# Centred context as 32-column weights, key weights split once for two context groups, three key banks, and a later store of the split context, in a two-layer attention and expert kernel

## The reference, cut to what matters

```python
# x, context: 16 batches of 128 rows, 512 wide
# L0 attention: q = layernorm(x), k = v = context, 16 heads, dh = 32
D = jnp.exp(log_D - max_log_D)                      # decays, lower triangle
C = (jnp.einsum('bhsd,bhtd->bhst', qh, kh) / jnp.sqrt(dh)) * D
normalizer = jnp.maximum(jnp.abs(C.sum(-1, keepdims=True)), jnp.exp(-max_log_D))
h = jnp.einsum('bhst,bhtd->bhsd', C / (normalizer + EPS), vh)
mu = h.mean(-1, keepdims=True)
var = ((h - mu) ** 2).mean(-1, keepdims=True)
hn = (h - mu) * jax.lax.rsqrt(var + EPS) * ln_scale
x = x + hn                                          # heads side by side
...
# L1 attention: keys of the context, 16 heads of 128, over all 16 batches
k_img = rms_norm(context @ ki_w + ki_b, nki_s)      # ki_w is 512 x 2048
```

## Time and profile before

| | |
|---|---|
| median of 3 runs (lowest, highest) | 1386.42 us (1383.04, 1388.37) |
| profiled execution, its own time | 1384.88 us |
| span in its trace, first to last instruction | 1383.2 us |
| PE, share of the span busy | 96% |
| DVE, ACT, POOL | 60%, 55%, 28% |
| heads stage in the trace | 194 to 492 us |

### The profile page before, as it was taken

The page is one execution under the profiler, slowest core; times in us unless marked ns, Lnnn a source line. Parts: engine busy times, 40 slices in busy tenths (PEclk is TensorE's granted clock), DMA queues, the critical chain, the costliest instruction groups (busy, mean ns, idle before and its releaser), DMA issues. The chain is left out here.

```text
span 1383.2 us, 24553 instructions
## 1 busy us (share of the span) xinstructions
PE 1324.5 (96%) x7326; PEld 1108.3 (80%) x7327; DVE 836.1 (60%) x1590; ACT 764.5 (55%) x1895; POOL 392.7 (28%) x374
## 2 busy tenths in 40 slices
PE   7899998999999989989998989999989999999998
PEld 6688877888888768778886778888878888888887
DVE  3645544567677865354444568635467777777965
ACT  4334457788887542154445545544577555555551
POOL 0111022374639004569631054027101000000041
PEclk9999998999999999999999999999999999999999
DMA  9984497888788567475656887474556655555413
GB/s 305 353 320 154 175 314 256 270 266 268 259 269 266 174 192 265 167 237 172 205 153 220 302 261 223 108 244 156 184 180 172 167 155 166 155 164 157 125 35 122
DMA packets 175095, 288.33 MB, mean 208 GB/s; under 512 B 30176, under 2 KB 64736, under 8 KB 174752
## 3 DMA queue, kind: packets, MB, share of 16 engines
q1 hardware_dynamic: 149200, 231.78, 53.3%
q0 software_dynamic: 8672, 29.37, 6.6%
q10 hardware_dynamic: 17136, 26.09, 5.2%
HBM read 178.38 MB, written 108.80 MB: 208 GB/s over the span
## 5 line engine op out<-in xcount | busy, mean ns | idle before, releaser
L120 PE MATMUL banks<-of_shared_split,key_lead 128*128 128x512 f32 x256 | 109.5, 428 | 10.5 <-ACT heads_ksq L1051 5.4
L2939 ACT ACTIVATE prob<-banks,attend_row,rq 128x128 f32<-128x128 f32 x248 | 110.5, 470 | 0.0
L2952 ACT ACTIVATE attend_ol<-banks,of_attend_vbias 128x512 fp32r<-128x512 f32 x64 | 44.2, 690 | 117.0 <-PE banks L3151 117.0
L120 PE MATMUL banks<-wo,attend_ol 128*128 (+1 forms) x256 | 106.2, 415 | 0.0
L122 PE MATMUL banks<-of_shared_split,key_trail 128*128 128x512 f32 x256 | 103.5, 404 | 0.0
L121 PE MATMUL banks<-of_shared_split,key_lead 128*128 128x512 f32 x256 | 103.2, 403 | 0.0
L120 PE MATMUL banks<-queries_rows_split,queries_wl 128*128 128x512 f32 x256 | 100.9, 394 | 0.0
L122 PE MATMUL banks<-wo,attend_ot 128*128 (+1 forms) x256 | 100.7, 393 | 0.0
L121 PE MATMUL banks<-wo,attend_ol 128*128 (+1 forms) x256 | 99.9, 390 | 0.0
L122 PE MATMUL banks<-queries_rows_split,queries_wt 128*128 128x512 f32 x256 | 99.8, 390 | 0.0
L121 PE MATMUL banks<-queries_rows_split,queries_wl 128*128 128x512 f32 x256 | 99.7, 390 | 0.0
(11 more groups left out here) (395 smaller groups left out, 3671.8 us busy)
## 6 DMA issues: line engine op xcount, KB each, us to landing
mlstm_gmax<-running_max SPq DMA_DIRECT2D x36, 512.0 KB, 6.5
key_raw<-in_L_xattn_ki_w SPq DMA_DIRECT2D x32, 512.0 KB, 6.4
k_heads<-heads_key ACTq DMA_DIRECT2D x64, 256.0 KB, 4.9
q_heads<-queries_head SPq DMA_DIRECT2D x64, 256.0 KB
q_ahead<-q_heads SPq DMA_DIRECT2D x64, 256.0 KB, 4.2
of_attend_k<-k_heads SPq DMA_DIRECT2D x60, 256.0 KB, 4.0
of_attend_v<-v_heads SPq DMA_DIRECT2D x60, 256.0 KB, 3.4
sorted_rows<-of_shared_split SPq DMA_DIRECT2D x2, 5120.0 KB, 29.6
```

The costliest lines, as they stand in the source:

```text
L120: nc.tensor.matmul(out, lead_l, lead_r, start=first, stop=False)
L2939: ins = nc.scalar.activation(prob[:, j % 2, b, :], ps[:, j % 2, b * S:(b + 1) * S], ACT.Exp, bias=row[:, j % 2, 1, b:b + 1], scale=rq[:, b ...
L2952: nc.scalar.activation(ol[:, par, j, :], ps[:, 4 + j % 2, :], ACT.Identity, bias=vbias[:, bass.ds(quad_of(it) * 4 + j, 1)]).then_inc(ol_do ...
```

## The change

1. *Outputs.* The context is centred ahead: DVE takes each head's mean over the 32 columns (`context_sum`), POOL subtracts it (`value`, now a subtraction), and since the centred columns add up to zero, the last of 32 is left out and holds ones in its place. The outputs of four heads are made at once at steps 2, 6, 10 and 14 (`outputs`): the context of one head and batch is the weight, 128 rows by 32 columns, and `cmat` streams past it; the four heads write the four strips of 32 partitions of bank 0. DVE copies the bank to `heads_hT` (`gather`), PE turns it back with four transposes at the next step (`turn_heads`), ACT copies it out (`quad`). `close` puts the left-out column back as minus the sum of the others. The subtraction of the mean behind the outputs is gone.
2. *Key order.* KEYS lists 64 units of (head, group, visit). Behind the first 8 units, two heads run for one group and the next before the weights change, so weights are split 40 times (VISITS), not 64, and read from DRAM 20 times, not 32. Seven of the first eight leading parts are made by POOL (`early_lead`). OPENING has new steps.
3. *Banks.* Keys use banks 6, 7 and 1; a unit waits for the square of the unit three before it.
4. *Loads.* The split context of groups 2 and 3 comes in a burst of eight at steps 14 and 15 of the body before. Context for the heads is loaded a body earlier.
5. *Values stage.* The four stores of the split context move to units 30, 32, 34 and 36.

```diff
@@ values_and_gates, SP
-                if u % 4 == 2 and u >= 6 and u < 6 + 4 * G:
-                    g = (u - 6) // 4
+                if u % 2 == 0 and 30 <= u < 30 + 2 * G:
+                    g = (u - 30) // 2
...
@@ heads_and_keys
-    OPENING = (0, 1, 3, 5, 7, 10, 12, 15)
+    OPENING = (0, 1, 2, 3, 6, 9, 12, 15)
...
+    KEYS = [(k % 2 * HALF + 2 * p + j, g, k * HALF + 2 * p + j)
+            for k in range(G + 1) for p in range(HALF // 2) for g in (k - 1, k) if 0 <= g < G for j in range(2)]
+    VISITS = HALF * (G + 1)
+    KEY_BANKS = (6, 7, 1)
...
@@ SP, body
-                    if n >= LAG and not last:
-                        A.load_split(sp, after(g, PER)[0], n - LAG)
+                    if first and n >= LAG:
+                        A.load_split(sp, 1, n - LAG)
+                    if not first and not last and n >= PER - 2:
+                        if n == PER - 2:
+                            sp.wait_ge(product, CLOSES[g - 1] + 1)
+                        for part in range(C):
+                            A.load_split(sp, g + 1, (n - PER + 2) * C + part)
...
@@ POOL
+                if b == 0:
+                    pool.wait_ge(cmean_done, count + 1)
...
+                ins = nc.gpsimd.tensor_tensor(ctx1[:, half(g), b, :, 0:LAST_E],
+                                              ctx[:, b, :].rearrange("p (h e) -> p h e", e=DH0)[:, :, 0:LAST_E],
+                                              piece(cmean, b).unsqueeze(2).broadcast_to([P, H0, LAST_E]), ALU.subtract)
...
+            def early_lead(g, m):
+                if m:
+                    pool.wait_ge(raw_loaded[m // 2 % 2], (m // 4 + 1) * 16)
+                    if m >= 2:
+                        pool.wait_ge(product, m - 1)
+                    nc.gpsimd.tensor_scalar(A.wl[:, m % 2], raw[:, m // 2 % 2, :, m % 2 * P:(m % 2 + 1) * P], 1.0, None,
+                                            ALU.mult).then_inc(wl_done, 1)
...
@@ ACT
-            def pair(g, k):
-                act.wait_ge(pv, g * PER + 2 * k + 2)
+            def quad(g, c):
+                act.wait_ge(quad_turned, g * QUADS + c + 1)
...
+                nc.scalar.activation(hraw[:, half(g), :, 4 * c:4 * c + 4, :].rearrange("p b j e -> p b (j e)"),
+                                     ps[:, 0, :].rearrange("p (b w) -> p b w", b=GB), ACT.Copy).then_inc(h_done, 1)
...
             def weight_lead(g, m):
...
+                if u == FIRST_OF[v] and v >= HALF:
+                    if v == HALF:
+                        act.wait_ge(wl_done, HALF)
+                    act.wait_ge(product, LAST_OF[v - 2] + 1)
+                    A.weight_lead(act, KEYS[u][0], v // 4)
...
@@ DVE
+            def context_sum(g, b):
...
+                nc.vector.tensor_reduce(piece(cmean, b), ctx[:, b, :].rearrange("p (h e) -> p h e", e=DH0), AX, ALU.add
+                                        ).then_inc(csum_done, 1)
...
+            def gather(g, c):
+                dve.wait_ge(pv, g * QUADS + c + 1)
+                if g or c:
+                    dve.wait_ge(quad_turned, g * QUADS + c)
+                nc.vector.tensor_copy(hT[:], ps[:, 0, :]).then_inc(ht_done, 1)
...
@@ PE
+            def outputs(g, c):
...
+                if g or c:
+                    pe.wait_ge(h_done, g * QUADS + c)
+                pe.wait_ge(c_done, g * PER + 4 * c + 4)
                 for b in range(GB):
+                    for j in range(4):
+                        ins = nc.tensor.matmul(ps[32 * j:32 * j + 32, 0, b * S:(b + 1) * S], ctx1[:, half(g), b, 4 * c + j, :],
+                                               cmat[:, j, b, :], start=True, stop=True)
                 ins.then_inc(pv, 1)
+
+            def turn_heads(g, c):
+                pe.wait_ge(ht_done, g * QUADS + c + 1)
+                for b in range(GB):
+                    ins = nc.tensor.transpose(ps[:, 0, b * P:(b + 1) * P], hT[:, b * S:(b + 1) * S], K.ident[:])
+                ins.then_inc(quad_turned, 1)
...
             def keys(g, m):
...
+                pe.wait_ge(wt_done, v + 1)
+                if u >= 3:
+                    pe.wait_ge(ksq_done, u - 2)
...
                     keys_at(g, n, 0, keys, first)
                     if n % 4 == 2:
                         scores(g, n + 2, first)
-                    outputs(g, n, first)
+                        outputs(g, n // 4)
+                    if n % 4 == 3:
+                        turn_heads(g, n // 4)
```

More of the change, by code:

```diff
@@ L950, in add @@
                     ins.then_inc(res_done, 1)
+            def early_lead(g, m):
[5 more added lines that the diff above has]
+                                            ALU.mult).then_inc(wl_done, 1)
             def body(g, first):
                 for n in range(PER):
+                    if first and n + 1 in OPENING:
+                        early_lead(0, OPENING.index(n + 1))
                     mask(g, n + AHEAD)
-                    if 5 <= n < 8:
-                        for b in ((0,), (1, 2), (3,))[n - 5]:
-                            value(after(g, PER)[0], g + 1, b)
+                    at = n - (9 if first else 5)
+                    if g + 1 < G and 0 <= at < 3:
+                        for b in ((0,), (1, 2), (3,))[at]:
+                            value(g + 1, g + 1, b)
                     if not first:
-                        for at, step in ((3, centre), (8, scale), (10, weigh), (12, add)):
+                        for at, step in ((8, scale), (10, weigh), (12, add)):
                             if at <= n < at + 2:
@@ L1080, in _ @@
             last = G - 1
-            pair(last, PAIRS - 1)
+            quad(last, QUADS - 1)
             row_sums(last)
@@ L1173, in body @@
                 for n in range(PER):
+                    if n % 4 == 3:
+                        gather(g, n // 4)
                     decayed(g, n + 1, first)
+                    at = n - (7 if first else 3)
+                    if g + 1 < G and at in (0, 1):
+                        context_sum(g + 1, 2 * at)
+                        context_sum(g + 1, 2 * at + 1)
                     keys_at(g, n, 1, weight_trail, first)
@@ L1204, in _ @@
             divisor(last)
-            mean(last, 0)
-            finish(PER - LAG + 1)
-            mean(last, 1)
-            dve.wait_ge(mean_done, G)
-            shift(nc.vector, last, 0)
-            finish(PER - LAG + 2)
-            for b in range(1, GB):
-                ins = shift(nc.vector, last, b)
-            ins.then_inc(centred, 1)
-            finish(PER - LAG + 3)
+            close(last, 0)
+            close(last, 1)
+            for m in range(1, 4):
+                finish(PER - LAG + m)
             dve.wait_ge(row_stats.summed, EARLY)
@@ L1267, in scores @@
                             ins.then_inc(qk, 1)
-            def outputs(g, n, first):
-                if n == 0:
+            def outputs(g, c):
+                if c == 0:
                     pe.wait_ge(ctx1_done, g + 1)
-                if n % 2 == 0 and not (first and n < 4):
-                    pe.wait_ge(h_done, g * PAIRS + n // 2 - 1)
-                pe.wait_ge(c_done, g * PER + n + 1)
+                if g or c:
+                    pe.wait_ge(h_done, g * QUADS + c)
+                pe.wait_ge(c_done, g * PER + 4 * c + 4)
```

175 lines of the change are left out of this document (85 added, 90 removed).

## The result

The changed kernel takes 1377.3 us (median of four runs, 1374.94 to 1379.30) beside 1387.4 of the kernel before, run with it. The ratio is 0.9937, with a 95% interval from 0.9916 to 0.9958: some 9 us faster, where 20 were forecast.

A forecast was written before the change was run, and what follows sets the result against it. PE was taken to bound the heads stage, except its opening, bound by a POOL, ACT and DVE chain. 1384.88 - 19.4 - 3.9 + 4.5 + 1.0 + 0 - 2.1 + 0 = 1365.1, predicted as a 1367 us median; range 1358 to 1390.

The forecast's parts named there:

- rival 2: Heads stage: the chain from transposes over ACT to the trailing part replaces the outputs as bound; about 1381 us, chance 0.21.
- Opening: First body of the heads stage: late second key unit against cheaper outputs and relieved ACT; taken as 0, bounds -8 and +6.
- Outputs: Outputs on PE in column strips plus transposes: 1.76 us gained a quad, 19.4 us in eleven quads.
- Rival 1: Outputs on PE: column strips run one after another, 34 us more, 1401; chance 0.14 with whatever else ends above 1390.
- Third key bank: PE's waits for a key's square all go: 5.4 us, 3.9 in the eleven quads and 1.5 in the tail.
- A new wait: Second key unit behind the transposes waits for its new weight: 1.5 us a body, 4.5 for three, bounds 0 and 18.
- Loads: Split context arriving in bursts: 0 to 3 us of waiting for each of two, taken as 0.5 each.
- Tail: Last eight key units: 1.5 us gained by the third bank, 0.6 by subtractions DVE is rid of; together -2.1.
- Stores: Later split-context stores in the values stage free nothing the early 4.70 us wait needs; taken as 0, bounds -6 and +3.
- the third: Sign that the prediction is wrong: the opening body lasts over 73 us.
- The second: Sign that the prediction is wrong: PE waits for split context at step 2 of a body for several microseconds.

The follow-up runs named there:

- out_twice: Changed kernel with PE making the outputs of every quad twice; ratio to the kernel before 1.0017, opening 77.2 us.
- act_opening_ctx: Changed kernel with early leading parts on ACT, opening steps of before, third group's context loaded at steps 12 to 15; ratio to the kernel before 0.9907.
- best: Changed kernel with leading parts on ACT, opening steps of before, third group's context loaded later, squares added one step later; 1361.3 us, ratio 0.9823.
- best_block: best with the third group's context loaded again at steps 8 to 11 of the first body; ratio to the kernel before 0.9856, opening 70.1 us.
- leads_act: Changed kernel with the leading parts of the first eight key weights made by ACT, none by POOL; ratio to the kernel before 0.9898.
- store_early: Changed kernel with the split context stored at units 6, 10, 14 and 18 of the values stage, as before; ratio to the kernel before 0.9958.

## Why the prediction was off

The direction and the mechanism on PE were right, the time lies within the range, and the size is less than half of what was forecast. That the time lies within the range is in part luck: 1377.3 falls into the band of rival 2 (1374 to 1390), whose mechanism did not happen. The step that failed is **Opening**, "I take 0, bounds -8 and +6": it measured +11.3. The prediction's terms add up to -19.9 (1365.0; it says 1365.1). With 11.3 more, the forecast would have been -8.6, beside a measured -8.7 (0.63%). So close a match says little: the interval of the ratio goes from -5.8 to -11.7 us, and the touched stages of the two traces differ by 1.8 + 11.3 - 17.4 + 0.8 - 0.4 = -3.9.

What the step said of the second key unit was right: it forecast 206.7 and 207.12 was measured, 11.0 us behind the first scores where 12.4 were forecast, with a stage that started 1.8 later. Two other parts were wrong. It set 7 us of cheaper outputs against the delay, though the prediction itself had said that PE waits for other engines there; out_twice shows that in the changed kernel's opening 4 us of outputs cost nothing that can be seen. And it stopped at the second unit. POOL's leading parts stand behind masks that wait for SP, and the third group's loads, moved into the first body, make SP wait for POOL's subtraction, which DVE's reductions make late; the step followed neither list. With the leading parts and the steps as before the change and the third group's loads four steps later, 10.3 of the 11.3 are gone (act_opening_ctx); with these loads alone back at step 8, the opening of best grows by 6.9 (best_block). ACT's relief, 4.3, did not pay for the move: with the leading parts back on ACT the opening is 7.1 shorter (leads_act).

The other terms:

- **Outputs**: 19.4 forecast; 2.14 x 11 = 23.5 came. The strips took 1.01 where 1.20 was taken, the transposes 0.35 for 0.44. Rival 1 (3.34) is refuted. The Trainium skill (TensorE: Matmul & The Clock Gate, Part 3, "Measured speedup vs the span model") led to 1.36 because its 2.38, which is for three column strips (at a stream of 512), was put in for four. Here four give 3.24 / 1.01 = 3.2, which agrees with it strip by strip: 0.80 each, against 2.38 / 3 = 0.79. The rule of the Trainium skill on weight loads (TensorE: Matmul & The Clock Gate, Part 3, "The mechanism"), which spoke for rival 1, does not hold back column strips: 32 records on the same 128 rows, in four column strips, take 1.01.
- **Third key bank**: the waits for a square are gone, as forecast (4.0 in the eleven quads by the waits of before). But 3.9 was the price in the old order. In the new one, where units follow one another more closely, the bank is worth 11.7, lower clock included.
- **A new wait**: 4.5 forecast for the weights behind the transposes; 0.5 was measured in the eleven quads. Rival 2 named this chain, and it didn't happen. A wait that no rival named took its place: the decayed scores, 6.6 where 0.5 stood before.
- **Loads**: 1.0 forecast for two bursts, 3.8 measured, within the bounds.
- These four together: the waits in the eleven quads were 7.5 and are 165.0 - 11 x 13.76 = 13.6, so 23.5 + 7.5 - 13.6 = 17.4. That is close to the forecast of 17.8 (19.4 + 3.9 - 4.5 - 1.0) because errors of both signs cancelled.
- **Tail**: -2.1 forecast, +0.8 measured from the last scores on; two waits for trailing parts, 2.8 in all, stand there.
- **Stores**: taken at 0, and store_early agrees. The early wait is still there, 4.57 in place of 4.70.

Of the signs named beforehand, the third failed: "if the opening body lasts over 73 us" the prediction is wrong, and it lasted 78.2. The second came near: PE waited 2.9 for the split context at step 2 of the third body.

## What to carry to other kernels

When a change hands work to an engine that was idle, follow that engine's whole list, and the list of the queue that issues its loads, up to the next point where the critical engine waits; an idle engine that works in order can still be late with everything behind one wait. A gain in a stage where the critical engine waits for others should be counted as nothing until the waits are followed through. And a delay can be hidden by another: undo the suspected causes together, then put them back one at a time, and judge by the sum of the stretches, since what one gains the next can lose.

## What was not expected of the hardware

Sixteen matmuls with weights of 128 rows by 32 columns and a stream of 128, in four column strips, take 1.01 us for 32 records, 32 ns each, against 0.81 / 8 = 101 ns for records that follow one another. Loads with a 32nd of the bytes (16 KB, not 512) landed 4.2 us behind their issue and not 5.4, by the median of eight, and POOL still waited 25.5 us for them, against 30.7.
